# A prologue of its own: two batches projected and stacked before the first maxima, loads on two queues

## The reference, cut to what matters

```python
qh = (q @ W_q).reshape(B, S, N_HEADS, HEAD_DIM)
kh = (k @ W_k).reshape(B, S, N_HEADS, HEAD_DIM)
vh = (v @ W_v + b_v).reshape(B, S, N_HEADS, HEAD_DIM)
...
keep = (j < i) | (i == 0) & (j == 0)
scores = jnp.where(keep, scores, jnp.float32(-jnp.inf))
probs = jax.nn.softmax(scores, axis=-1)
attn = jnp.einsum('bhij,bjhd->bihd', probs, vh).reshape(B, S, HID)
return attn @ W_o + b_o
...
x = x + _L0_xattn_ref(_layernorm(x, axis=-1), ctx_1024, ctx_1024, ...)
x = x + _L0_ffn_ref(_layernorm(x, axis=-1), ...)
```

## Time and profile before

| | |
|---|---|
| median of three runs | 482.71 us (481.94 to 484.05) |
| profiled execution | 487.3 us, of which the span is 485.6 us |
| TensorE busy | 383.3 us (79%) |
| DVE, GpSimd, ScalarE busy | 294.2, 226.6, 187.5 us |
| granted TensorE clock, mean | 0.899 of full speed |

### The profile page before, as it was taken

How to read it: one execution, slowest core, us unless ns; L and a number is a source line. 1 busy time by engine, 2 the same in 40 slices (tenths; PEclk the granted TensorE clock), 3 DMA queues, 4 the chain that set the end, 5 groups by cost and what they waited for, 6 DMA issues and landing times. The chain is left out here.

```text
span 485.6 us, 8107 instructions
## 1 busy us (share of the span) xinstructions
PE 383.3 (79%) x3026; PEld 323.5 (67%) x3026; DVE 294.2 (61%) x614; ACT 187.5 (39%) x255; POOL 226.6 (47%) x311
## 2 busy tenths in 40 slices
PE   0557588988889899887732289999999999999970
PEld 0444467676767677665621169999989898989860
DVE  2535356767676766741229696677777777686540
ACT  1412254645454545346114052535353525252310
POOL 4581964747474746324012780444453536250504
PEclk9957899999999999987555589999999999999995
DMA  7620563616060608231210250454544637240403
GB/s 190 192 84 12 152 170 73 172 27 174 26 174 24 174 3 213 62 133 38 104 43 1 66 216 22 130 144 152 120 169 99 194 79 208 65 51 1 44 1 43
DMA packets 35736, 49.10 MB, mean 101 GB/s; under 512 B 4735, under 2 KB 31537, under 8 KB 34673
## 3 DMA queue, kind: packets, MB, share of 16 engines
q1 hardware_dynamic: 27744, 35.42, 24.0%
q0 software_dynamic: 6272, 8.57, 9.6%
q10 hardware_dynamic: 1680, 4.60, 3.0%
HBM read 27.57 MB, written 8.39 MB: 74 GB/s over the span
## 5 line engine op out<-in xcount | busy, mean ns | idle before, releaser
L1143 POOL DMA_INDIRECT out_dram<-Y,scatter_idx x32 | 51.9, 1623 | 109.0 <-DVE Y L1294 101.7
L1185 ACT ACTIVATE hr<-ps,b_sb 128x512 f32<-128x512 f32 x64 | 43.4, 688 | 108.9 <-PE ps L1353 74.1
L594 DVE TENSOR_REDUCE nm<-ps 128x2 f32<-128x512 f32 (+1 forms) x96 | 61.9, 683 | 22.0 <-PE ps L753 22.0
L1363 PE MATMUL ps<-w_hi,h_hi 128*128 128x256 f32 x256 | 72.9, 285 | 2.0 <-DVE h_lo L1276 2.0
L1363 PE MATMUL ps<-w_lo,h_hi 128*128 128x256 f32 x256 | 72.4, 283 | 0.0
L1363 PE MATMUL ps<-w_hi,h_lo 128*128 128x256 f32 x256 | 72.4, 283 | 0.0
L422 ACT ACTIVATE PT<-ps 128x1536 f32<-128x1536 f32 x32 | 46.4, 1449 | 28.2 <-PE ps L767 27.8
L1274 DVE CAST h_hi<-hr 128x512 fp32r<-128x512 f32 x64 | 29.1, 454 | 43.4 <-ACT hr L1185 43.3
L1353 PE MATMUL ps<-XT_hi,w_hi 128*128 128x512 f32 x128 | 51.2, 400 | 1.5 <-DVE XT_lo L1263 1.5
L1363 PEld LDWEIGHTS ps<-w_hi,h_hi 128*128 128x128 f32 x256 | 48.9, 191 | 4.1 <-DVE h_lo L1276 2.4
L1353 PE MATMUL ps<-XT_hi,w_lo 128*128 128x512 f32 x128 | 50.9, 397 | 0.0
(11 more groups left out here) (174 smaller groups left out, 839.0 us busy)
## 6 DMA issues: line engine op xcount, KB each, us to landing
raw<-in_L_ffn_w_dram SPq DMA_DIRECT2D x12, 1024.0 KB, 7.8
raw<-in_L_ffn_w_dram ACTq DMA_DIRECT2D x4, 1024.0 KB, 5.5
Qs<-q_h SPq DMA_DIRECT2D x24, 128.0 KB, 2.4
Ks<-k_h SPq DMA_DIRECT2D x24, 128.0 KB, 2.5
c_sb<-in_ctx_dram SPq DMA_DIRECT2D x8, 256.0 KB, 2.7
Qs<-q_m SPq DMA_DIRECT2D x16, 128.0 KB, 2.5
Ks<-k_m SPq DMA_DIRECT2D x16, 128.0 KB, 2.5
xn_rows<-x2n SPq DMA_DIRECT2D x8, 256.0 KB, 2.4
```

Of the source, the lines that this page charges most:

```text
L594: dve.tensor_reduce(nm[:, tile, h:h + count], max_bank[u % 2].rearrange("p (h j) -> p h j", h=count), AX_X, ALU.max, negate=True).then_inc ...
L1143: pool.indirect_dma_start(out_rows[:, :], bass.IndirectOffsetOnAxis(ap=scatter_idx[q][:, j:j + 1], axis=0), Y[q][:, j, :], None, bounds_ch ...
L1185: act.activation(hr[c % 2][:, :], h_bank[c % 4], ACT.Relu, bias=b1_sb[q][:, c:c + 1]).then_inc(hr_ready, 1)
L1363: last = pe.matmul(y_bank[j // 2][:, (j % 2) * D:(j % 2 + 1) * D], a[c % 4][:, j * P:(j + 1) * P], w[q][:, c, :], start=(c == 0 and n == 0 ...
```

## The change

The pipeline's prologue is written out for each engine, apart from `steps`, which now starts at step 0:

- TensorE projects batch 0 and batch 1 back to back (queries, keys and values of batch 0, then queries and keys of batch 1) and only then runs the maxima of batch 0. Batch 0's projections go to banks 3, 4 and 5 (`first_bank`). The value projection of batch 1 stays in step 0.
- ScalarE's queue loads Wq and Wk. SyncE's loads x and context of batches 0 and 1 and Wv, then the biases and router weights; Wo and the rest of x are issued when Wv has landed. The context buffer `c_sb` is doubled, and each refill is issued one step earlier.
- GpSimd makes the masks first and issues no DMA in the prologue; the fills of `Qs[0]`, `Qs[1]` and `Ks[0]` are DVE's, the other three GpSimd's. Bias addition for x and the constants of the routing come at the prologue's end.
- In step 0, the first `b_scores` moves on TensorE from behind the value projection to behind the third pair of maxima units, and ScalarE's two roundings of batch 2's queries and keys move ahead of the first and second exponential.

Steps from 1 on keep their instructions and order.

```diff
+    first_bank = [ps[:, 3, :], ps[:, 4, :], ps[:, 5, :]]
...
+    c_sb = [sb(f"c_sb{q}", [P, 2, S], F32) for q in range(2)]
...
+    def query_bank(s):
+
+        return first_bank[0] if s == -2 else bank[1]
+
+    def key_bank(s):
+
+        return first_bank[1] if s == -2 else bank[0]
+
+    def values_bank(s):
+
+        return first_bank[2] if s == -1 else bank[0]
...
+            def load_context(n):
+                sp.dma_start(c_sb[n % 2][:, :, :], ctx_tiles[n]).then_inc(ctx_loaded[n % 2], 16)
+
             sp.dma_start(x_all[:, 0:2, :], x_tiles[:, 0:2, :]).then_inc(x0_loaded, 16)
-            sp.dma_start(c_sb[:, :, :], ctx_tiles[0]).then_inc(ctx_loaded, 16)
-            sp.dma_start(w_raw[:, 0], Wq.rearrange("(k p) n -> p k n", p=P)).then_inc(wqkvo_loaded[0], 16)
-            sp.dma_start(w_raw[:, 1], Wk.rearrange("(k p) n -> p k n", p=P)).then_inc(wqkvo_loaded[1], 16)
+            load_context(0)
+            sp.dma_start(x_all[:, 2:4, :], x_tiles[:, 2:4, :]).then_inc(x1_loaded, 16)
             sp.dma_start(w_raw[:, 2], Wv.rearrange("(k p) n -> p k n", p=P)).then_inc(wqkvo_loaded[2], 16)
+            load_context(1)
+            sp.dma_start(bv_bc[:, :], bv.rearrange("(a n) -> a n", a=1).broadcast_to([P, D])).then_inc(small_loaded, 16)
+            sp.dma_start(bo_bc[:, :], bo.rearrange("(a n) -> a n", a=1).broadcast_to([P, D])).then_inc(small_loaded, 16)
+            sp.dma_start(wg_sb[:, :, :], wg.rearrange("(k p) e -> p k e", p=P)).then_inc(small_loaded, 16)
+            sp.wait_ge(wqkvo_loaded[2], 16)
             sp.dma_start(w_raw[:, 3], Wo.rearrange("(k p) n -> p k n", p=P)).then_inc(wqkvo_loaded[3], 16)
-            sp.dma_start(x_all[:, 2:, :], x_tiles[:, 2:, :]).then_inc(x_loaded, 16)
+            sp.dma_start(x_all[:, 4:, :], x_tiles[:, 4:, :]).then_inc(x_loaded, 16)
...
-                if proj_part and s + 3 < B:
+                if s + 4 < B:
                     sp.wait_ge(cT_lo_ready, s + 3)
-                    sp.dma_start(c_sb[:, :, :], ctx_tiles[s + 3]).then_inc(ctx_loaded, 16)
-                if proj_part:
+                    load_context(s + 4)
...
         def _(pool):
-            pool.dma_start(bv_bc[:, :], bv.rearrange("(a n) -> a n", a=1).broadcast_to([P, D])).then_inc(small_loaded, 16)
-            pool.dma_start(bo_bc[:, :], bo.rearrange("(a n) -> a n", a=1).broadcast_to([P, D])).then_inc(small_loaded, 16)
-            pool.dma_start(wg_sb[:, :, :], wg.rearrange("(k p) e -> p k e", p=P)).then_inc(small_loaded, 16)
             pool.memset(ident[:, :], 1.0).then_inc(const_tmp, 1)
...
+            mask_constants()
+            norm_powers(0)
+            buffer_constants(0)
+            split_context(-2)
+            norm_powers(1)
+            fill_keys(1)
+            split_queries(-2)
+            split_keys(-2)
+            split_context(-1)
+            split_queries(-1)
+            split_keys(-1)
+            norm_powers(2)
+            fill_keys(2)
+            zero_queries(2)
+            buffer_constants(1)
+            add_bias(0)
+            add_bias(1)
+            routing_constants()
+            steps(step)
             pool.wait_ge(const_tmp, 15)
 
...
         def _(act):
+            act.dma_start(w_raw[:, 0], Wq.rearrange("(k p) n -> p k n", p=P)).then_inc(wqkvo_loaded[0], 16)
+            act.dma_start(w_raw[:, 1], Wk.rearrange("(k p) n -> p k n", p=P)).then_inc(wqkvo_loaded[1], 16)
...
+                    if s == 0:
+                        round_queries(s)
+                        exp(s, 0)
+                        round_keys(s)
+                        exp(s, 1)
+                    elif score_part(s):
+                        exp(s, 0)
+                        exp(s, 1)
+                    if proj_part(s) and s > 0:
...
             norm_x(0)
             round_weights(1)
-            steps(act, step)
+            round_context(-2)
+            round_x(-2)
+            norm_x(1)
+            round_weights(2)
+            round_queries(-2)
+            round_keys(-2)
+            round_x(-1)
+            round_context(-1)
+            round_queries(-1)
+            round_keys(-1)
+            norm_x(2)
+            round_weights(3)
+            copy_maxima(-1)
...
+            dve.wait_ge(x0_loaded, 16)
+            norm_stats(x_all[:, 0:2, :], st1, mv1, ln1_stats, 0)
+            dve.memset(Ks[0][:, :, :].rearrange("p h t -> p (h t)").bitcast(F32), ONES).then_inc(k_filled[0], 1)
+            split_weights(0)
+            next_stats(-2)
+            split_weights(1)
+            split_x(-2)
+            dve.memset(Qs[1][:, :, :].rearrange("p h t -> p (h t)").bitcast(F32), 0.0).then_inc(q_zeroed[1], 1)
+            split_weights(2)
+            split_queries(-2)
+            split_keys(-2)
+            split_x(-1)
+            add_value_bias(-1)
+            split_queries(-1)
+            split_keys(-1)
+            next_stats(-1)
+            split_weights(3)
+            dve.memset(x2n[:, :, :], 0.0).then_inc(x2n_stored, 16)
+            for pair in range(UNITS // 2):
+                maxima(-1, pair)
+            split_maxima(-1)
+            steps(step)
...
+                if s == 0:
+                    project_values(s)
+                    turn_x(s)
+                    a_scores(s, 0)
+                    a_scores(s, 1)
+                    queries(s)
+                    a_scores(s, 2)
+                    b_scores(s, 0)
+                    keys(s)
+                    a_scores(s, 3)
+                    b_scores(s, 1)
+                    a_scores(s, 4)
+                    values(s, 0)
+                    b_scores(s, 2)
+                    a_scores(s, 5)
+                    values(s, 1)
+                    b_scores(s, 3)
+                    turn_maxima(s)
+                    values(s, 2)
+                    values(s, 3)
...
+            turn_x(-2)
+            queries(-2)
+            keys(-2)
+            project_values(-1)
+            turn_x(-1)
+            queries(-1)
+            keys(-1)
+            for pair in range(UNITS // 2):
+                a_scores(-1, pair)
+            turn_maxima(-1)
+            steps(step)
 
```

More of the change, by code:

```diff
@@ L516, in step @@
[L516 to L526 removed]
+                    if proj_part(s):
+                        round_context(s)
@@ L730, in _, with maxima @@
-            steps(dve, step)
+            def maxima(s, pair):
+                for u in (2 * pair, 2 * pair + 1):
+                    dve.wait_ge(a_done, UNITS * (s + 1) + u + 1)
+                    if u == 0 and not first(s, 0):
+                        dve.wait_ge(nm_ready, 2 * (s + 1))
+                    tile, h, count = max_unit(u)
+                    dve.tensor_reduce(nm[:, tile, h:h + count], max_bank[u % 2].rearrange("p (h j) -> p h j", h=count),
+                                      AX_X, ALU.max, negate=True).then_inc(max_done, 1)
@@ new lines, in b_scores @@
+            def b_scores(s, g):
+                if g == 0:
+                    pe.wait_ge(max_stacked, 16 * (s + 1))
+                    if s == 0:
+                        pe.wait_ge(v_ready, 1)
+                if not (first(s, 1) and g == 0):
+                    pe.wait_ge(exp_done, GROUPS * s + g)
+                for hh in range(HPG):
+                    h = HPG * g + hh
+                    pe.matmul(prob_score[:, hh * S:(hh + 1) * S], Ks[s % BUFS][:, h, 0:P], Qs[s % BUFS][:, h, :], start=True, stop=True)
+                for hh in range(HPG):
+                    h = HPG * g + hh
+                    last = pe.matmul(prob_score[:, HPG * S + hh * P:HPG * S + (hh + 1) * P], Ks[s % BUFS][:, h, P:S], Qs[s % BUFS][:, h, P:S],
+                                     start=True, stop=True)
+                last.then_inc(b_done, 1)
@@ new lines, in turn_values @@
+            def turn_values(s, t):
+                if t == 0:
+                    pe.wait_ge(ot_ready, 2 * s)
+                    if not (s > B - 1):
+                        pe.wait_ge(nmT_ready, s + 1)
+                elif max_part(s):
+                    pe.wait_ge(v_ready, s + 2)
+                elif not score_part(s):
+                    pe.wait_ge(lg_ready, s - 1)
+                for g in range(GROUPS):
+                    last = pe.transpose(bank[1 - t][:, g * P:(g + 1) * P], OT[:, g, t * P:(t + 1) * P], ident[:, :])
+                last.then_inc(ott_done, 1)
@@ new lines, in project_turned @@
+            def project_turned(to, n, hi, lo, done):
+                for f in range(2):
+                    m = 0
+                    for k in range(2):
+                        for w, a in ((w_hi, hi), (w_lo, hi), (w_hi, lo)):
+                            m += 1
+                            last = pe.matmul(to[:, f * S:(f + 1) * S], w[:, n, k, f * P:(f + 1) * P], a[:, k, :],
+                                             start=(m == 1), stop=(m == 6))
+                last.then_inc(done, 1)
@@ new lines, in project, with queries @@
+            def project(to, n, hi, lo, done):
+                for t in range(2):
```

(29 more changed lines are left out.)

979 lines of the change are left out of this document (422 added, 557 removed).

## The result

The changed kernel is slower: 485.43 us median of 12 runs (483.68 to 487.69), against 482.45 us for the kernel before on the same chip (12 runs, 480.49 to 484.05). The ratio is 1.0062, with a 95% interval of 1.0043 to 1.0082. The forecast was 479.4 us, with a range of 476.5 to 482.7. The profiled execution took 483.68 us, with a span of 481.9 us and a granted clock of 0.913; it was the fastest of the twelve.

The account below looks back on a forecast made before the run. The prediction took the start of step 1 on TensorE, 75.13 us, as what the change could move. Step 1 at 71.2 (-3.9 us) plus 0.6 for clock gave -3.3 us: median 482.7 to 479.4 us, range 476.5 to 482.7.

Parts of the forecast that it names:

- The base: Starting time for the sum: profiled execution 487.3 us becomes 484.0, so the median 482.7 becomes 479.4.
- Part 1: Loads at the head: Wq lands below 6.4 us, normalising of batch 0's x starts at about 7.0, -5.1 us.
- Part 2: Prologue: DVE's split of Wk clashes with GpSimd's context subtraction and delays xT_lo and the query projection, +1.0 us.
- Landing: Batch 0's stacking copies land at 25.0 us instead of 29.1, releasing k_h for batch 1's key rounding.
- Part 3: From batch 0's stack landing to DVE's first maximum: 7.7 us of queued work, first maximum at 32.7 against 32.77.
- Part 4: Step 0, from the small transpose at 42.7 to step 1's start at 71.2, with batch 1 already stacked: -3.9 us.
- Clock: TensorE in step 0: half of one 3.4 us stretch at the 1.2 GHz level, 0.35 us lost per us, +0.6 us.
- Low clock through step 0: Rival, 8 in 100: TensorE at 1.2 GHz for 18 us of step 0, net +2.4 us, 485.1 us; decides from 11 us.
- Loads no sooner: Rival, 15 in 100: Wq lands at 10.6 us or later, first maximum at 36 or so, time 482 to 483.3 us.

Follow-up runs that it names:

- e1: The kernel before, unchanged, profiled and timed a second time: 482.04 us, ratio 0.9994.
- e9: Changed kernel with DVE's first weight split moved behind the statistics of batch 1, the fill of Ks[0] staying: 483.93 us, ratio 1.0051.
- e2: Changed kernel with DVE's fill of Ks[0] moved behind the first xT_lo: 483.50 us, ratio 1.0011 to the kernel before.
- e7: Kernel before with only the new load queues (Wq, Wk on ScalarE; biases and router weights on SyncE): 481.65 us, ratio 1.0002.
- e3: Changed kernel with DVE's split of Wo and fill of x2n moved behind batch 0's maxima: 480.69 us, ratio 0.9977 to the kernel before.
- e10: Changed kernel with TensorE and ScalarE running step 0 in the old order, prologue still changed: 476.53 us, ratio 0.9891 to the kernel before.
- e13: Changed kernel with TensorE's and ScalarE's old step 0 order, Ks[0] fill behind first xT_lo, Wo split and x2n fill behind the maxima: 469.25 us.
- e14: Changed kernel with TensorE's and ScalarE's old step 0 order and GpSimd's splits of batch 2 ahead of the second mask: 477.66 us, ratio 0.9910.
- e4: Changed kernel with GpSimd's splits of batch 2 moved ahead of the second mask in step 0: 480.67 us, ratio 0.9964 to the kernel before.

## Why the prediction was wrong

Against the typical head of before (e1), the changed kernel's step 1 starts 75.53 - 72.65 = 2.9 us later, which is the 3.0 us between the medians. It is made of +0.8 up to x of batch 0, +4.8 from there to the first maximum, -0.2 for the maxima, and -2.6 in step 0.

The forecast had -3.3 us and +3.0 were measured. The marks account for these 6.3 us: 2.5 from the base, 2.7 from the normalising of x, -0.2, +0.2 and -0.6 on the way from there to the transpose, and 1.7 from step 0 (30.8 against 28.5 and the clock's 0.6). So two steps failed most: the base, and the start of the normalising at 7.0.

- **The base.** "487.3 becomes 484.0, and the median of the runs, 482.7, becomes 479.4" failed. It took the 4.6 us by which the profiled execution lay above the median for an offset that the change would leave alone. But that execution held a late head (step 1 at 75.13, in the other two profiles at 72.65 and 73.18) and a rest 4 us longer, and no timed execution of that kernel took over 484.7 us. So most of the waiting that Part 1 was to remove is not there in a usual execution. Against its own base the forecast even looks right (484.0, measured 483.68), but that is luck: step 1 starts 3.7 us later than forecast, and the rest is 4.1 us shorter.
- **Part 1, loads.** "Wq should be there by 4 to 6 us": right, 4.47. "The normalising then starts at about 7.0": wrong, 9.66. With Wq early, GpSimd's factors were late next, and they were late because of the new loads: DVE's subtraction was ready while the fill ran. e9 and e2 show it with 7.27 and 7.58: without that wait the 7.0 would have been nearly right. Against the typical 8.83 the -5.1 us are +0.8, and even 7.0 would have been no more than -1.8.
- **Part 2, the clash.** It was priced at +1.0 and cost DVE nothing: both operations started at 11.87, `w_lo` took 0.66 and GpSimd's `cT_lo` 1.79. GpSimd paid 0.5 us (`cT_lo` takes 1.27 in e7). The row that gave the price had GpSimd first, at 15.56 against 15.65. In the twelve profiles of kernels with the new prologue both start at the same time to 0.01 us, and each time DVE's subtraction takes 0.66 us and GpSimd's 1.78 or 1.79. In these traces DVE pays where one of its subtractions comes while GpSimd's runs, as the second one in e9.
- **Landing.** 25.0 forecast; `k_h` was released at 27.43, late by the 2.7 us of x.
- **Part 3.** The step was right: 7.7 forecast, 35.35 - 27.43 = 7.9 measured, and the split of Wo and the fill stand last in it. What was wrong was to book it as "given back to 0.1": it ate more than the head had, since the head had nothing. e3 shows that 5.5 us of it could be had back.
- **Part 4, step 0.** Forecast 28.5 us from the transpose to step 1, measured 30.8: the first exponential came 10.8 us behind the transpose (9.3 forecast), `k_l` ended at 22.9 (21.2), and step 1 came 7.9 us behind that (7.3). So 1.5 of the 2.3 us arise ahead of the first exponential. In sign it was right: before, step 0 takes 32.3 to 33.5. The larger fault is what the step left out. It followed the new order of TensorE and ScalarE row by row, and never priced the old one on the new head. With the new prologue, batch 1 stacked early, and the old order, step 0 is 33.4 - 22.6 = 10.8 us shorter (e1 and e10), and in the changed kernel the new order takes 8.2 of them. A part of both numbers is the clock, whose grant in step 0 is 0.85 in e1, 1.00 in e10 and 0.81 in the changed kernel.
- **Clock.** +0.6 stood for half a stretch of 3.4 us at 1.2 GHz. The changed kernel's step 0 has three stretches at that level (PEclk is the third number from the end):

```profile
50.30:53.70 3.40, 3.18 (x18) 3.00 (x19) 1.76 (x3) 0.00 (x0) 0.00 (x0) 0.53 0.20 63
60.60:64.00 3.40, 3.18 (x30) 1.88 (x29) 1.56 (x3) 1.45 (x1) 1.36 (x3) 0.54 0.02 5
70.80:75.53 4.73, 3.00 (x33) 1.43 (x33) 0.00 (x0) 1.66 (x2) 1.47 (x4) 0.50 0.85 168
```

  They are 11.5 us in all, just past the 11 from which the second rival was to decide. At the prediction's 0.35 they would be worth 4.0 us, but step 0 is only 2.3 us longer than its sum for full clock. That rival, *Low clock through step 0*, had the sign and with 485.1 the nearest number, in part by luck: the head's 2.7 us and the base are not in it. With the old order the grant in step 0 was 1.00 in e10, but 0.93 and 0.86 in e13 and e14, so the low stretches can't be put down to the new order alone.
- **Loads no sooner** did not occur: Wq was rounded at 4.47, not as late as before. Its mark, a first maximum at 36 or so, nearly did (35.35), by GpSimd's wait. The change did what it says.
- Steps from 1 on: the rest is 406.4 us in the changed kernel and in e1, as forecast.

## What to carry to other kernels

Profile the kernel before twice before a wait of its first microseconds is priced: three executions of one kernel had the same load ready at 8.3, 8.7 and 11.6 us. When a change moves work and rewrites the order around it, price both on their own; here the move was worth 10.8 us in step 0 and the order around it cost 8.2, some 3 us of it without any help of the clock (e4 and e14). The early place in an order belongs to what feeds the longest chain of other engines: with the first scores behind three pairs of maxima units on TensorE, and a 0.6 us rounding ahead of each of the first two exponentials on ScalarE, the second mask and the splits came 8 to 9 us later. Which of these two engines' orders counts for more was not tested, since they were moved together.
